# First attention: row maxima from the 40 rows of high parts, the two heads of a pair on two halves of TensorE's rows

## The reference, cut to what matters

```
q = concatenate([q_content, q_rope], -1)                     # 8 + 32 = 40
k = concatenate([k_content, k_rope], -1)
scores = einsum('bhqd,bhkd->bhqk', q, k) / sqrt(40)
scores = where(causal, scores, -inf)
attn = softmax(scores, -1)
out = einsum('bhqk,bhkd->bhqd', attn, v) ... @ W_o
```

## Time and profile before

| | |
|---|---|
| median of 3 runs | 1750.57 us |
| the profiled execution: its own time | 1747.28 us |
| its span, from the first to the last instruction | 1745.5 us |
| first matmul of `mx` / last | at 67.3 us / 915.3 us |
| TensorE busy in the stretch 67 to 915 us | 699.55 of 848 us |
| VectorE busy there | 610.02 us |
| ScalarE busy there | 375.43 us |
| granted clock of TensorE there | 0.94 of 2.4 GHz |

### The profile page before, as it was taken

One profiled execution on the slowest core, in us unless ns is written; L12 is line 12 of the kernel. 1 busy time (PEld: TensorE's weight loads), 2 busy tenths in 40 slices (PEclk: granted clock), 3 DMA queues, 4 the chain that ended last, 5 costly groups with the idle time before them and its releaser, 6 DMA issues.

```text
span 1745.5 us, 36985 instructions
## 1 busy us (share of the span) xinstructions
PE 1377.1 (79%) x13404; PEld 896.9 (51%) x13404; DVE 1127.0 (65%) x3630; ACT 703.9 (40%) x1139; POOL 688.7 (39%) x1004
## 2 busy tenths in 40 slices
PE   3487888878888888787886799959899984877881
PEld 2243434444344444443544566637677773665671
DVE  4477686776767767777673554438888775444556
ACT  1044444534444444444453033425544441113673
POOL 3022232232332332323222123357976763564664
PEclk9699999989999989999898699968988885556996
DMA  4645616356164461553702401111221112112334
GB/s 103 94 79 83 100 24 106 57 87 99 24 102 64 73 111 20 86 88 54 125 11 99 142 28 33 40 44 52 56 60 34 33 34 97 33 38 73 89 89 160
DMA packets 74151, 123.23 MB, mean 71 GB/s; under 512 B 17680, under 2 KB 46359, under 8 KB 73076
## 3 DMA queue, kind: packets, MB, share of 16 engines
q1 hardware_dynamic: 65252, 106.81, 32.2%
q0 software_dynamic: 7616, 13.59, 2.3%
q10 hardware_dynamic: 1104, 0.48, 0.1%
HBM read 30.47 MB, written 17.60 MB: 28 GB/s over the span
## 4 chain that ended last, share of the span: by engine, by line
PE 54%; DVE 21%; issue 6%; DMA 6%; SPq 5%; ACT 4%; POOL 3%; DVEq 0%; ACTq 0%; POOLq 0%
PE S L548 5%; DVE first L760 5%; PE A L577 5%; PE S L1016 4%; SPq L484 4%; PE S L540 4%; PE S L559 4%; PE S L1336 3%; DVE S L765 3%; PE A L1347 3%; PE S L168 2%; DMA Kp<-rck 2%; DVE tB L742 2%; PE S L1353 2%; PE A L1028 2%
## 5 line engine op out<-in xcount | busy, mean ns | idle before, releaser
L653 ACT ACTIVATE P<-S 128x1024 f32<-128x1024 f32 (+3 forms) x384 | 309.7, 809 | 406.1 <-PE S L559 403.0
L836 POOL TENSOR_SCALAR_AFFINE_SELECT P<-P 128x256 f32<-128x256 f32 (+1 forms) x256 | 115.0, 450 | 502.0 <-ACT P L653 501.9
L548 PE MATMUL S<-Kp,Qp 120*128 120x512 f32 (+3 forms) x768 | 241.8, 400 | 73.3 <-DMA Kp<-rck 43.7
L559 PE MATMUL S<-Qp,Kp 121*128 121x512 f32 (+3 forms) x768 | 239.5, 396 | 66.0 <-DVE first L760 21.7
L765 DVE CUSTOM_DVE_ANT_0 S<-S,later 128x512 f32<-128x512 f32 (+3 forms) x512 | 239.6, 513 | 59.3 <-PE S L548 58.2
L548 PEld LDWEIGHTS S<-Kp,Qp 120*128 120x128 f32 x768 | 130.3, 201 | 217.6 <-issue 101.5
L760 DVE TENSOR_REDUCE first<-S 128x2 f32<-128x1024 f32 x128 | 156.6, 1223 | 111.3 <-PE S L548 110.7
L559 PEld LDWEIGHTS S<-Qp,Kp 121*128 121x128 f32 x768 | 134.5, 199 | 139.9 <-DVE first L760 39.9
L577 PE MATMUL A<-P,V 128*9 128x512 f32 (+3 forms) x1536 | 183.9, 526 | 3.7 <-POOL P L836 3.7
L1558 POOL TENSOR_TENSOR prod<-qf,kT 128x128 f32<-128x128 f32 x160 | 78.5, 524 | 29.4 <-PE A L1347 22.2
L1984 POOL DMA_INDIRECT yq<-yq,id x71 | 69.6, 980 | 51.4 <-DVE yq L1939 34.7
(11 more groups left out here) (316 smaller groups left out, 2786.7 us busy)
## 6 DMA issues: line engine op xcount, KB each, us to landing
Qp<-rcq SPq DMA_DIRECT2D x64, 256.0 KB
Kp<-rck SPq DMA_DIRECT2D x64, 256.0 KB
Qp<-rcq SPq DMA_DIRECT2D x64, 128.0 KB
Kp<-rck SPq DMA_DIRECT2D x64, 128.0 KB
xq<-xq SPq DMA_DIRECT2D x71, 72.0 KB, 1.9
yb<-yq SPq DMA_DIRECT2D x8, 528.0 KB, 4.8
Qp<-cq SPq DMA_DIRECT2D x64, 64.0 KB
Kp<-ck SPq DMA_DIRECT2D x64, 64.0 KB
```

What stands on the lines that cost most here:

```text
L548: ins = te.matmul(S[s][:, 512 * h:512 * h + n], Q[0:120, h, 128 * qt:128 * qt + 128], K[0:120, h, 512 * part:512 * part + n], start=True, ...
L559: ins = te.matmul(S[s][:, 512 * h + c:512 * h + 512], K[0:121, h, 128 * kb:128 * kb + 128], Q[0:121, h, 512 * qh + c:512 * qh + 512], star ...
L653: se.activation(k.P[(w.n - 1) % NP0][:, :, c:512], S[s][:].rearrange("p (j k) -> p j k", j=2)[:, :, c:512], ACT.Exp, scale=SCALE0).then_in ...
L836: ge.affine_select(P[:, :, start:c + 128], P[:, :, start:c + 128], [[0, 2], [1, wide]], ALU.is_ge, 0.0, base=start - c, channel_multiplier ...
```

## The change

The matmuls of `mx` use the 40 rows of high parts alone, so the maximum that is subtracted before the exponential is that of the high-by-high product. The same shift stands in the sums and in the normalisation, so the result of the softmax is kept. For the first head of a pair these rows stay at 64 to 103. For the second head they are moved to rows 0 to 39, and its rope rows from 0 to 63 to 40 to 103; the rows from 104 on stay. So the matmul of the first head uses rows in the upper half of the array's 128 rows (64 to 127), and that of the second head rows in the lower half (0 to 63). Each of the two still writes its own 512 columns of the slot. The number and size of the DMAs, the semaphores, the number of instructions and their order on every engine stay as they are. Line numbers behind line 314 move up by one, and by two behind line 481.

```diff
@@ -312,6 +312,7 @@
 LAG = 4
 NP0 = 6
 NU = 8 * B
+HIGH = (64, 0)
 EARLY = 3
@@ -478,8 +479,9 @@
             for h in range(2):
                 r, q = 16 * (2 * u % 8 + h), 8 * (2 * u % 16 + h)
                 rope, content = k.RH[name][r:r + 16].bitcast(F32), k.CH[name][q:q + 8].bitcast(F32)
-                for at, many, src in ((64, 2, rope[:, high]), (96, 1, content[:, high:high + 1]), (104, 2, content),
-                                      (0, 4, rope.rearrange("p a b t -> p (a b) t"))):
+                z = HIGH[h]
+                for at, many, src in ((z, 2, rope[:, high]), (z + 32, 1, content[:, high:high + 1]), (104, 2, content),
+                                      (40 * h, 4, rope.rearrange("p a b t -> p (a b) t"))):
                     rows = dst[at:at + many * src.shape[0], h, :].bitcast(F32)
                     ye.dma_start(rows, src).then_inc(p.sem(f"d_q{u % 4}").h, 16)
@@ -545,8 +547,8 @@
             pe.wait_ge(p.sem("g_ones"), 1)
             shipped(p, pe, u)
             for h in range(2):
-                ins = te.matmul(S[s][:, 512 * h:512 * h + n], Q[0:120, h, 128 * qt:128 * qt + 128],
-                                K[0:120, h, 512 * part:512 * part + n], start=True, stop=True)
+                r = slice(HIGH[h], HIGH[h] + 40)
+                ins = te.matmul(S[s][:, 512 * h:512 * h + n], Q[r, h, 128 * qt:128 * qt + 128], K[r, h, 512 * part:512 * part + n], start=True, stop=True)
             ins.then_inc(p.made("mx").h, 1)
```

## The result

| | before | after |
|---|---|---|
| median, 4 runs each | 1748.65 us | 1811.86 us |
| lowest to highest | 1743.32 to 1753.07 | 1797.51 to 1820.16 |
| ratio to before, 95% interval | | 1.0354 [1.0276, 1.0433] |
| span of the profiled execution | 1745.5 us | 1815.2 us |
| first to last matmul of `mx` | 67.3 to 915.3 us | 69.6 to 985.4 us |

The forecast was 1759 with a range of 1738 to 1790. The direction was as forecast, the size was not. All but 2 us of it lies between the first and the last `mx`: this stretch grew by 67.9 us to 916, past the 875 that the prediction named as its bound, and what follows did not move. Lines 548, 559, 577, 760 and 765 of before are 551, 561, 579, 762 and 767 now.

The account below looks back on a forecast made before the run. The prediction took TensorE and VectorE as a coupled pair bounding the stage. Changes of 24.7 us less 30.5 of streams on the chain gave -5.8; plus 14 off it, +8 on 1750.6: 1759 us, range 1738 to 1790.

Parts of the forecast that it names:

- the 875 that the prediction named as its bound: Stretch from first to last `mx`, 848 us before: the forecast is wrong if it ends under 842 or over 875.
- Pairing: The two `mx` matmuls on separate halves stream and load together, saving 30.5 us of streams on the chain.
- Rival (b): In `mx`, the halves' loads go one behind the other, second matmul 0.107 us late: 1778 us, chance 0.17.
- The price of a change: On TensorE around `mx`, switching between whole array and halves costs 0.215 us at full clock, against 0.01 without.
- Rival (a): Around `mx`, a change between whole array and halves is free: 1731 us, chance 0.15.
- The sum at the old clock: First to last `mx`: chain and off-chain terms together add 8 us, with the granted clock held at 0.92 to 0.95.
- -5.8 for the chain: On the old chain of waits: 24.7 us of arrangement changes less 30.5 us of saved `mx` streams.
- +14 for what falls behind off it: Of 42 us of arrangement changes off the old chain, 0 to 17 come on the path; taken as 14.
- the sum of the uncovered changes: At 327 new places around `mx` the wait is too short to hide the arrangement change: shortfalls of 66.6 us.
- The clock: TensorE's granted clock between the first and last `mx` stays within 0.92 and 0.95; before it was 0.94.
- rival (c): Granted clock falls between first and last `mx`: 24% at half clock instead of 12%, 20 us more, 1779 us; chance 0.12.
- the prediction's own formula: Cost of added half-clock time in the stage: that time times TensorE's share of the chain, halved (100 x 0.4 / 2 = 20 us).

Follow-up runs that it names:

- the second profile of the new kernel: The changed kernel (40 + 40 rows, two halves) run once more against the kernel before: median 1800.24 us, ratio 1.0324, stage 896 us.
- the other order: `mx` items two by two ahead of each `pv`: against the kernel before, 1.0183 with its 120 rows, 1.0239 with the changed kernel's 40 + 40.

## Why the prediction was wrong

**Pairing: right.** The two matmuls and their two loads go together, 3 to 4 ns apart. Rival (b) is out.

**The price of a change: right.** 0.10 of emptying and 0.12 of a load at full clock, also between the whole array and a half. Rival (a) is out.

**The sum at the old clock: too high by some 20 us.** It was -5.8 for the chain and +14 for what falls behind off it, +8 in all. The thirteen units at an unchanged clock went from 338.2 to 334.1 us, -4; over the stage the line gives -17, and -11 for the second profile of the new kernel. The 14 us are not there; the chain's own sum was the better estimate. At the old clock the change would thus have made the kernel a little faster. That the direction came out as forecast is luck: the clock, which the forecast held still, made it slower. In counting, the clock's levels had been laid 10 us off the matmuls. Laid right, 68 instead of 70 us of streams are saved, and the sum of the uncovered changes moves by less than 5 us, which alters nothing here.

**The clock: the step that failed.** The prediction kept the clock at 0.92 to 0.95. It held "TensorE stays busy for 80% of this one" against rival (c), gave it 0.12, and sized it as 24% at half clock and 20 us. Rival (c) is what happened, four times as large. The clock fell to 0.80: 375 of 916 us at half clock, 41%, 279 us more than before, and at 0.30 us for each of them, not 0.20, that is 84 us.

The busy share was the wrong thing to look at: it rose, from 82% (700 of 848) to 88% (806 of 916), while the clock fell. What the argument lacked was the cost of using 40 rows in place of 120, which it set at nothing. The runs show this as a cause by itself: 120, 72 and 65 rows in the old arrangement have 96, 219 and 272 us at half clock, with nothing else changed. The changes of arrangement, which the prediction priced by their own time alone, are the second cause (272 and 424 us for 65 and 64 rows, and 256 for 324 or 375 with fewer changes in the new kernel), though the first of these pairs also leaves half of the rows unused. Fewer streams lower the clock too in the old kernel (96 to 167), but in the new one twice the streams did not bring it back.

The price per microsecond was low for a reason of its own. The prediction took TensorE's share of the chain over the whole stage, 40%, and so 0.20 us. The half-clock time lies where TensorE holds the chain, for 82% of it; by the prediction's own formula that would be 0.41, and the line gives 0.30.

**Shown and not shown.** That the added time lies in the stretches at half clock is shown unit by unit; that fewer rows lower it is shown by kernels that differ in nothing else, but for the values in the rows. That more changes lower it rests on the step from 65 to 64 rows, with the rival named there, and on the other order, where the order itself has a price. How rows, streams and gaps add up to the granted clock is open. Rows times the time they stream do not give it: the new kernel with its pairs doubled has as many half-clock microseconds (362) as without, and 120 rows for one head alone have 167, where 65 rows for both have 272. That it is the gaps in the changes, rather than something else in them, that lower the clock was not tried alone.

## What to carry to other kernels

A matmul with few rows takes no less time than one with many (386.2 against 388.5 us in the fifteen units with 72 rows at an unchanged clock), but in this kernel it lowered the clock for everything around it: before cutting the rows of a matmul, or laying two of them side by side, look at the granted clock of the stage (here 0.94, so it already fell at times), and compare it, and the durations of unchanged matmuls, before and after. Pairing on two halves has a price where the neighbours have another arrangement: between matmuls of the whole array each item pays 0.215 us twice. No run here has neighbours of the same arrangement, so what pairing gives there is not shown. Busy share does not tell how near the clock is to falling. And what a slower clock costs goes by TensorE's share of the chain where the clock is low, not by its share of the whole stage.

## What was not expected of the hardware

- Rows in use, at equal columns and order, move the granted clock: 0.94, 0.88, 0.85 in the stage for 120, 72 and 65 rows (one profile each; every run's clock over the whole execution agrees), and 2.4 to 2.5% of time.
- Leaving out half of the `mx` matmuls saves nothing that the runs can tell (0.9976 [0.9943, 1.0008]): the clock fell from 0.94 to 0.90.
- One row less, 64 instead of 65, costs 69 us; from there on TensorE changes its arrangement at each item.
- Two full-width loads of weights to the two halves of rows take 0.19 us together, as long as one.
